# Cross-attention chain of four layers: where the key units, the weighted-norm waves, the Newton steps and one exponential stand in an eight-step order

## The reference

```
q = heads(x @ Wq[l]);  k = heads(ctx @ Wk[l]);  v = heads(ctx @ Wv[l])
p = softmax(q k^T / sqrt(8))                 # layers 0 to 2, over all 77 rows (see below)
x = x + (p v) @ Wo[l] + bo[l]
# layer 3: the 73 text rows and the 4 image rows have a softmax each
p_t = softmax(q k_text^T / sqrt(8))
qsem = l2norm(p_t @ ctx_text);  sem = qsem . l2norm(ctx_image)
p_i = softmax(q k_image^T / sqrt(8) + 0.5 * sem) * fside
x = x + (p_t v_text + p_i v_image) @ Wo[3] + bo[3]
```

## Time and profile before

| what | value |
|---|---|
| median of three runs | 2267.34 us |
| profiled execution, its own time | 2264.95 us |
| its span | 2263.2 us |
| PE busy | 2086.4 us (92%) |
| DVE busy | 1481.7 us (65%) |
| ACT busy | 1075.1 us (48%) |
| POOL busy | 458.7 us (20%) |
| chain that ended last | PE 78%, SP's queue 8%, DVE 5%, issue 4% |
| mean granted TensorE clock | 0.970 |

### The profile page before, as it was taken

The page is one execution under the profiler, slowest core; times in us unless marked ns, Lnnn a source line. Parts: engine busy times, 40 slices in busy tenths (PEclk is TensorE's granted clock), DMA queues, the critical chain, the costliest instruction groups (busy, mean ns, idle before and its releaser), DMA issues.

```text
span 2263.2 us, 75842 instructions
## 1 busy us (share of the span) xinstructions
PE 2086.4 (92%) x26394; PEld 1697.5 (75%) x26394; DVE 1481.7 (65%) x4449; ACT 1075.1 (48%) x2733; POOL 458.7 (20%) x870
## 2 busy tenths in 40 slices
PE   2699999999999999999999999999999999999975
PEld 1567877887787788778778877887887788778764
DVE  3236776777677676767767766776676677667654
ACT  0245554455445455544545554554554455555431
POOL 0112122212212221221222122122212222222110
PEclk9889999999999999999999999999999999999975
DMA  3111111211111121112111111211211121111000
GB/s 82 49 43 50 52 43 42 52 50 39 47 52 44 41 52 51 38 46 52 45 41 52 52 38 47 53 44 40 52 52 38 47 53 44 39 53 38 22 10 5
DMA packets 108576, 101.31 MB, mean 45 GB/s; under 512 B 42240, under 2 KB 84952, under 8 KB 108184
## 3 DMA queue, kind: packets, MB, share of 16 engines
q1 hardware_dynamic: 104556, 92.88, 15.1%
q10 hardware_dynamic: 3628, 3.33, 0.6%
HBM read 34.13 MB, written 5.41 MB: 17 GB/s over the span
## 4 chain that ended last, share of the span: by engine, by line
PE 78%; SPq 8%; DVE 5%; issue 4%; DMA 2%; ACT 2%; ACTq 1%; DVEq 0%; POOLq 0%; POOL 0%
PE ps_s L738 11%; PE ps_c L816 10%; PE ps_s L771 8%; PE ps_c L886 6%; PE ps_k L839 6%; PE ps_k L644 5%; PE ps_q L717 5%; PE ps_c L875 4%; PE ps_k L670 4%; PE ps_s L788 4%; PE ps_k L844 4%; SPq L584 3%; PE ps_c L891 3%; PE ps_c L852 2%; SPq L577 2%
## 5 line engine op out<-in xcount | busy, mean ns | idle before, releaser
L1131 DVE TENSOR_REDUCE top<-ps_s 128x6 f32<-128x462 f32 (+3 forms) x1024 | 511.3, 546 | 88.2 <-PE ps_s L738 84.3
L1027 ACT ACTIVATE p_t<-ps_s 116x512 f32<-116x512 f32 (+1 forms) x768 | 372.9, 545 | 48.9 <-PE ps_s L771 46.9
L738 PE MATMUL ps_s<-k_blocks,q_sb 32*128 32x231 f32 (+1 forms) x3584 | 347.8, 384 | 20.3 <-issue 18.5
L816 PE MATMUL ps_c<-p_t,v_rows 116*27 116x128 f32 (+1 forms) x7168 | 288.7, 284 | 14.8 <-DMA v_rows<-v_img 12.3
L738 PEld LDWEIGHTS ps_s<-k_blocks,q_sb 32*128 32x128 f32 x3584 | 229.9, 185 | 84.9 <-issue 31.3
L816 PEld LDWEIGHTS ps_c<-p_t,v_rows 116*27 116x27 f32 (+1 forms) x7168 | 214.1, 108 | 86.5 <-issue 49.3
L1055 ACT ACTIVATE o_t<-ps_c 128x256 f32<-128x256 f32 x256 | 98.1, 383 | 368.3 <-PE ps_c L875 302.7
L1354 POOL TENSOR_TENSOR k_blocks<-k_sb,mask_k 128x231 f32<-128x231 f32 x384 | 211.8, 573 | 267.6 <-PE ps_s L771 252.5
L771 PE MATMUL ps_s<-q_sb,k_blocks 32*116 32x128 f32 (+1 forms) x5376 | 223.8, 283 | 27.7 <-DMA q_sb<-top_t 15.0
L839 PE MATMUL ps_k<-gram,p_t 116*128 116x154 f32 x896 | 210.6, 317 | 41.6 <-DVE weighted L1171 41.6
L771 PEld LDWEIGHTS ps_s<-q_sb,k_blocks 32*116 32x116 f32 (+1 forms) x5376 | 186.3, 175 | 63.7 <-issue 52.0
(11 more groups left out here) (118 smaller groups left out, 3595.3 us busy)
## 6 DMA issues: line engine op xcount, KB each, us to landing
v_rows<-v_img SPq DMA_DIRECT2D x128, 227.4 KB
context<-in_ctx SPq DMA_DIRECT2D x64, 336.0 KB, 3.0
q_sb<-top_t SPq DMA_DIRECT2D x576, 6.0 KB
v_rows<-v_img SPq DMA_DIRECT2D x64, 115.2 KB
v_rows<-v_img SPq DMA_DIRECT2D x64, 112.2 KB
v_rep<-v_dram SPq DMA_DIRECT2D x64, 50.0 KB
q_sb<-top_t SPq DMA_DIRECT2D x192, 2.0 KB
gram<-g_img SPq DMA_DIRECT2D x64, 46.3 KB
```

The source lines that it names most:

```text
L738: ins = pe.matmul(ps_s[:, z * 512 + j * GT:z * 512 + j * GT + n], q_sb[c % 3][lo:lo + QUAD, j * S:(j + 1) * S], k_blocks[c % 3][lo:lo + QU ...
L816: ins = pe.matmul(ps_c[t % 2][32 * (g % 4):32 * (g % 4) + UC, g // 4 * S:(g // 4 + 1) * S], v_rows[b % NC][0:n, v:v + UC], p_t[c % 3][0:n, ...
L1027: act.activation(to, source, ACT.Exp, scale=SCALE).then_inc(p_ready, 1)
L1131: dve.tensor_reduce(top[c % 2][:, z * BH:z * BH + m], s.rearrange("p (h t) -> p h t", t=T)[:, :, 0:n], AX.X, ALU.max).then_inc(s_top, 1)
```

## The change

The order of the units in the eight steps is altered; no arithmetic is.

- Keys: class 2 has none any more. In class 0 there are two units, `u=0` before the turned maxima and the second scores (layer 1 at `t%8==0`, layer 2 at `t%8==4`) and `u=1` behind the turning back, as before (layer 3 and layer 0). Each has its own pair of semaphores. `u=1`, and the image tokens, wait for the reading of `u=0`.
- Waves: in class 2, wave 2 stands before the second scores and wave 3 behind the turning back, as waves 0 and 1 do in class 1.
- VectorE: image steps 8 to 15 go from behind `results` to ahead of it in class 0, and 16 to 18 come from class 1 to the same place.
- ScalarE: `image_exp` goes ahead of all four `exps` in class 1; in class 3 the last of the four `text_exps` goes behind `exps` and `values_rest`.

```diff
-def keys_at(t):
-    if t % 8 == 4:
-        return 0, (t + 4) // 8
-    if t % 8 == 2:
-        return 1, (t - 2) // 8
-    if t % 8 == 6:
-        return 2, (t - 6) // 8
-    if t % 8 == 0:
-        return 3, (t - 8) // 8
+def keys_at(t, u):
+    if t % 8 == 0:
+        return [(1, t // 8), (3, (t - 8) // 8)][u]
+    if t % 8 == 4:
+        return [(2, (t - 4) // 8), (0, (t + 4) // 8)][u]
     return 0, -1
...
-            def keys(k, t):
+            def keys(k, t, u):
...
-                if e_six(t):
-                    pe.wait_ge(six_evac, raised(k, e_six, t))
-                else:
+                if k is None or u == 0:
                     units_done(k, t - 1)
+                if u == 1:
+                    pe.wait_ge(k_evac[0], raised(k, E_KEYS[0], t))
+                    if e_six(t):
+                        pe.wait_ge(six_evac, raised(k, e_six, t))
...
             def image_tokens(k, t):
                 units_done(k, t - 1)
+                pe.wait_ge(k_evac[0], raised(k, E_KEYS[0], t))
...
# TensorE, step
-                if e_waves(t) and t % 4 == 1:
+                if e_waves(t):
                     gram_wave(k, t, 0)
-                if e_keys(t) and t % 4 == 2:
-                    keys(k, t)
+                if E_KEYS[0](t):
+                    keys(k, t, 0)
                 if e_six(t):
                     image_tokens(k, t)
                 if topped(t):
                     turn_top(k, t)
                 if exists(t - 1):
                     second(k, t - 1)
-                if e_waves(t) and t % 4 == 2:
-                    gram_wave(k, t, 0)
                 if exists(t - 2):
                     turn_back(k, t - 2)
                 if e_waves(t):
                     gram_wave(k, t, 1)
-                if e_keys(t) and t % 4 == 0:
-                    keys(k, t)
+                if E_KEYS[1](t):
+                    keys(k, t, 1)
...
# ScalarE, step
-                if e_keys(t) and t % 4 == 2:
-                    keys(k, t)
+                if E_KEYS[0](t):
+                    keys(k, t, 0)
                 if e_six(t):
                     image_tokens(k, t)
                 if topped(t):
                     tops(k, t)
                 if ip(t):
-                    for i in range(4):
+                    for i in range(3):
                         text_exps(k, t, i)
-                for i in range(2):
-                    if exists(t - 1):
-                        exps(k, t - 1, i)
                 if ip(t - 6):
                     image_exp(k, t - 6)
-                for i in range(2, 4):
-                    if exists(t - 1):
+                if exists(t - 1):
+                    for i in range(4):
                         exps(k, t - 1, i)
-                if e_keys(t) and t % 4 == 0:
-                    keys(k, t)
+                if E_KEYS[1](t):
+                    keys(k, t, 1)
                 if e_values(t):
                     values_rest(k, t)
+                if ip(t):
+                    text_exps(k, t, 3)
...
# VectorE, step
-                if e_waves(t) and t % 4 == 1:
+                if e_waves(t):
                     weigh(k, t, 0)
                 if ip(t - 5):
                     norms(k, t - 5)
                     image_branch(k, t - 5, 1, 8)
-                if ip(t - 6):
-                    image_branch(k, t - 6, 16, 19)
                 if out(t):
                     new_x(k, t)
-                if e_waves(t) and t % 4 == 2:
-                    weigh(k, t, 0)
+                if ip(t - 5):
+                    image_branch(k, t - 5, 8, 19)
                 if ip(t - 6):
                     image_branch(k, t - 6, 19, 21)
                     image_weights(k, t - 6)
                 if exists(t - 2):
                     results(k, t - 2)
                 if e_waves(t):
                     weigh(k, t, 1)
-                if ip(t - 5):
-                    image_branch(k, t - 5, 8, 16)
```

More of the change, by code:

```diff
@@ L188, in e_values, with keys_in @@
     return 0 <= values_batch(t) < B
-def e_keys(t):
-    return 0 <= keys_at(t)[1] < B // 2
+def keys_in(u):
+    return lambda t: 0 <= keys_at(t, u)[1] < B // 2
+E_KEYS = [keys_in(u) for u in range(2)]
 def e_gram(t):
@@ L373, in build @@
         w_order = sem("w_order")
-        k_psum = sem("k_psum")
-        k_evac = sem("k_evac")
+        k_psum = [sem(f"k_psum{u}") for u in range(2)]
+        k_evac = [sem(f"k_evac{u}") for u in range(2)]
         k_ready = sem("k_ready")
@@ L429, in build @@
         block = ctx.enter_context(nc.Block())
-        primed = [k_psum, k_evac, k_ready, v_psum, va_evac, vb_psum, vb_evac, g_psum, g_evac, sq_ready,
+        primed = k_psum + k_evac + [k_ready, v_psum, va_evac, vb_psum, vb_evac, g_psum, g_evac, sq_ready,
                   sum_ready, six_psum, six_evac, n2_ready, vip_ready, q_psum, q_evac, s_psum, s_top,
@@ L510, in next_context @@
             def next_context(k, b, t):
-                sp.wait_ge(k_psum, raised(k, e_keys, t - 5))
+                sp.wait_ge(k_psum[1], raised(k, E_KEYS[1], t - 5))
                 at = b % NC * 2 * CX
@@ L621, in units_done @@
                 if k is None or t % 4 == 0:
-                    pe.wait_ge(six_evac, raised(k, e_six, t))
-                    pe.wait_ge(k_evac, raised(k, e_keys, t))
+                    pe.wait_ge(k_evac[1], raised(k, E_KEYS[1], t))
                 if k is None or t % 4 in (1, 2):
@@ L627, in units_done @@
                     pe.wait_ge(six_evac, raised(k, e_six, t))
-                    pe.wait_ge(k_evac, raised(k, e_keys, t))
-            def keys(k, t):
-                l, p = keys_at(t)
+                    pe.wait_ge(k_evac[0], raised(k, E_KEYS[0], t))
+            def keys(k, t, u):
+                l, p = keys_at(t, u)
                 if l == 0:
@@ L645, in keys @@
                                         start=kt == 0, stop=kt == 1)
-                ins.then_inc(k_psum, 1)
+                ins.then_inc(k_psum[u], 1)
             def image_tokens(k, t):
                 units_done(k, t - 1)
+                pe.wait_ge(k_evac[0], raised(k, E_KEYS[0], t))
                 pe.wait_ge(ld_six, raised(k, e_six_load, t, per=32, first=0))
@@ L828, in gram_wave @@
                     pe.wait_ge(p_ready, raised(k, exists, c, per=4))
[L829 to L832, removed]
+                    units_done(k, t - 1)
                 else:
@@ L959, in _, with keys @@
             act.wait_ge(setup, N_SET + 2)
-            def keys(k, t):
-                l, p = keys_at(t)
-                act.wait_ge(k_psum, raised(k, e_keys, t))
+            def keys(k, t, u):
+                l, p = keys_at(t, u)
+                act.wait_ge(k_psum[u], raised(k, E_KEYS[u], t))
                 act.wait_ge(k_ready, raised(k, exists, t, per=2))
@@ L967, in keys @@
                                ps_k[:, 0:4 * T].rearrange("p (a t) -> p a t", t=T)[:, :, 0:n],
-                               ACT.Identity, bias=minus[:, 0:1]).then_inc(k_evac, 1)
+                               ACT.Identity, bias=minus[:, 0:1]).then_inc(k_evac[u], 1)
             def image_tokens(k, t):
@@ L1346, in keys @@
                 l, b = layer(c), batch(c)
-                made = [u for u in range(c - 20, c) if keys_at(u) == (l, b // 2)]
-                pool.wait_ge(k_evac, raised(k, e_keys, made[0]))
+                made = [(t, u) for t in range(c - 20, c) for u in range(2) if keys_at(t, u) == (l, b // 2)]
+                pool.wait_ge(k_evac[made[0][1]], raised(k, E_KEYS[made[0][1]], made[0][0]))
                 if l == L - 1:
```

## The result

The changed kernel took 2302.6 us (median of four runs, 2296.9 to 2306.91) against 2268.12 us for the kernel before beside it (2263.43 to 2269.44): ratio 1.0166, 95% interval 1.014 to 1.0192. It is slower, as forecast, but by 34 us and not by 14, and 2302.6 lies above the range (2243 to 2299). Two things make up most of the 20 us between forecast and result: VectorE's results came later than priced, and TensorE's clock fell in the step with image tokens. The profiled execution took 2299.34 us (span 2297.6, mean granted clock 0.963), 34.4 above the one of before, so the two traces can be set against each other.

What follows compares the result with a forecast made beforehand. PE, 92% busy, was taken as bound by stalls, with ScalarE's exponentials and SP's queue nearly as tight. Nine rounds at +1.4 us (12.6) plus 1.7 outside gave +14: 2281 us, range 2243 to 2299.

Steps and rivals of the forecast that it cites:

- Keys `u=0`, 1.05: Class 0: the added unit of keys takes 1.05 us of PE, so the first scores end 1.05 later.
- SP stall of 0.29 in class 2: Class 2: SP's DMA issuing shifts 1.41 later, so PE's second scores wait for `move_top`, a new stall of 0.29 us.
- Exponentials bind classes 1, 2 and 3: ScalarE's exponentials hold PE's first scores, which end 1.10 us behind them; classes 1 and 3 shorten by 0.15 and 0.16.
- VectorE in class 0: Eleven small steps before `results` take 2.6 us; GpSimd blocking taken as 0.3 us, 0.29 free behind SP's stall, nothing added.
- VectorE late: Rival: GpSimd blocks several moved steps, results 0.9 us late for PE's turning; +33 us, 2314, or 2297 with half; chance 0.14.
- Image-token step, 1.91: Step `t%24==12`: image tokens wait 0.86 us for the keys' reading on top of 1.05, SP shifts 1.91; net +0.64 us.
- Class 3 and the loop's edge: Class 3: one fewer `text_exps` ahead saves 0.16 us; at the loop's edge exponentials don't bind it, so that group costs +0.28.

Runs made afterwards that it cites:

- experiment 1: Changed kernel with VectorE's image steps 14 to 18 put back behind `results` in class 0; 2287.56 us, 1.0095 of the kernel before.
- experiment 6: Changed kernel with image steps 14-18 behind `results`, Gram DMAs a step later, image-token-step keys early, plus half the layer-1 exponentials' columns left out; 2194.68 us, 0.9721 of before.
- experiment 2: Changed kernel with keys `u=0` right behind the product, ahead of the output projection, in the image-token step alone; 2278.06 us, 1.0059 of the kernel before.

## Why the prediction was right in direction and wrong in size

Two steps of the prediction failed: the lateness of VectorE's results in class 0, taken as 0.3 us and added as nothing, and the image-token step, priced as if the clock stayed up. Measured per round against forecast per round, it is +3.6 against +1.4; the 2.2 us between them, times nine, are 20 of the 20 us missed. Outside the loop it is +1.8 where I had 1.7.

- *Keys `u=0`, 1.05.* Right in kind, 1.14 to 1.15 in every plain class 0. +0.2 a round over the forecast, with the step at the loop's edge.
- *SP stall of 0.29 in class 2.* The mechanism is right, and experiment 1 shows it with 0.39. In the changed kernel it is mostly not seen, since class 1 comes late: 17 waits where I had some 60.
- *Exponentials bind classes 1, 2 and 3.* Right: 1.09 behind the last exponential in class 2, 7.30 for class 1 when nothing else is late, 8.00 for class 3; experiment 6 takes 0.64 off the one and gets 0.64 off the other.
- *VectorE in class 0: "I take 0.3", hidden by the SP stall, so "I add nothing".* This is the first step that failed. Not lengthened, eleven steps would have been the 2.6 us I took: from the first at 910.78 to `results` at 914.14 are 3.36, less 0.69. But in 25 of 36 plain groups three steps and not one were lengthened, and PE waited 0.65 and not 0.3; in the other 11 one step was, and PE waited some 0.2. I had counted "one of eight steps" against it. Read more closely, the rows said less: GpSimd's 1.10 us began at 890.48, and up to 891.03 VectorE was at `results`, which reads `ps_c`; only what was left of it met the image steps, of which the one at 890.95 kept its 0.17 and the next took 0.46. The wide steps came at 892.52 and later, when GpSimd was done, so no row of theirs beside GpSimd existed. The page "SBUF — State Buffer" of the Trainium skill, section "SBUF: two separate sides", has a rule for this (the shared port pair is held for the whole instruction), which I had cited and then priced below; the trace agrees with it, 0.41 to 0.50 against 0.23 to 0.24. Against the forecast the lateness costs 0.92 us a round in the four plain groups, net of the SP stall that it hides: 8 us in all (experiment 1 gives 0.85 a round). It is the mechanism of the rival "VectorE late", at about a quarter of the 33 us that I had given it.
- *Image-token step, 1.91.* The second step that failed. The wait is right (0.88 against 0.86), and the step without a lowered stretch is at 11.15, 2.18 more than before. But the granted clock falls in eight of nine, and the mean is +3.78. Against the forecast this is +1.87, of which 1.6 come with the clock. The long step takes 0.9 back in step 14 by hiding SP's stall, which leaves 0.96 a round, 9 us. None of my rivals had it.
- *Class 3 and the loop's edge.* +0.2 a round over the forecast. Class 3 gave its 0.19 in four of six steps. In step 19, at the edge, the time rose by 0.14; in step 7 it stayed (8.31 to 8.32). There, in step 103 of the kernel before, PE's second scores wait 0.26 us for VectorE, and the exponentials already followed them by 0.77.

The rows of the kernel before that the item on VectorE rests on, beside the earlier trace rows, of VectorE and then of GpSimd:

```profile
890.70 0.33 DVE L1192 TENSOR_TENSOR o_sb<-ps_c,recip 128x168 f32<-128x168 f32 x1
...
892.52 0.24 DVE L1242 TENSOR_TENSOR z_b<-z_a,rs_y 128x80 f32<-128x80 f32 x1
```

```profile
891.54 0.20 POOL L1377 TENSOR_TENSOR ip_n<-n_six,no_ip 128x4 f32<-128x4 f32 x1
```

All parts together: 0.92 + 0.96 + 0.2 + 0.2, less 0.1 in the group at the edge, is the 2.2.

The direction was not luck. With VectorE in time (experiment 1) the kernel is still slower than before, 1.0095 [1.0068, 1.0122], by waits that the forecast had priced: its round is +1.26 where the forecast had +1.4, with one lowered stretch behind the wait.

What stays open: why the clock falls behind the same wait in 1 to 8 of nine rounds, and at the loop's edge in some kernels at all eight passages and in others at two. The runs show that it does not fall there without the wait; that the wait alone brings it is not shown, as experiment 2 moves the keys with it. An added wait at that place in the kernel before was not tried.

## What to carry to other kernels

When small operations of VectorE are moved to another place, look at what GpSimd runs there, line its operations up with the steps one by one, and price each step that meets one at the lengthened time (here 0.4 to 0.5 us for 0.24), not at the share that was lengthened at the old place; and look for the next engine in line with less slack than the delay. Price a new PE wait in a nearly full stretch with the chance that the granted clock falls behind it: here 0.9 us of wait became 1.1 us without a lowered stretch and 2.7 with one (4.4 where it was twice as long). And where a queue issues 13.5 us without a gap, try to move what nobody waits for soon out of that stretch: four DMAs moved by themselves went with 22 us less, some 16 of them in the steps where the queue had been late.

## What the hardware showed that I had not expected

The granted clock fell to 0.5 for 3.4 us after a PE wait of only 0.88 us, in the middle of work, and in one round each of three kernels for 6.8; PE had been busy 5.72 of 6.60 us ahead of it. At the loop's edge it also falls, at all eight passages in the kernel before and at two to seven in the others, mostly at 1 to 2 us each, while executions of one kernel spread as widely as the smaller parts of this change are worth (2272 to 2292 in experiment 1).
